# Local attention: scaling the queries on POOL with the keys, and a new order of copies and projections

## The reference, cut to what matters

```
h = shift_token(x)                       # half of the features from the token before
q, k, v = split(h @ wqkv)                # 8 heads of 64
q = l2norm(q) * qs;  k = l2norm(k) * ksc
q, k = rotary_xpos(q, k)                 # q*cos*scale + rotate_half(q)*sin*scale; k with 1/scale
...
sim = (8 * q) @ k.T                      # each window sees itself and the window before
attn = softmax(where(mask, -max, sim))
x = x + (attn @ v) @ wo
h = shift_token(x)
mu = h.mean(-1);  var = h.var(-1)        # for the feed-forward half that follows
```

## Time and profile before

| what | us |
|---|---|
| median of 3 runs | 1599.19 |
| profiled execution, its own time | 1601.15 |
| its span in the profile | 1599.4 |
| first local attention, start to the end of its last copy | 742.1 to 1084.1 |
| second local attention | 1163.6 to 1506.3 |
| PE busy / DVE busy / ACT busy / POOL busy, whole span | 1303.0 / 1178.1 / 1009.1 / 787.2 |

### The profile page before, as it was taken

One profiled execution on the slowest core, in us unless ns is written; L12 is line 12 of the kernel. 1 busy time (PEld: TensorE's weight loads), 2 busy tenths in 40 slices (PEclk: granted clock), 3 DMA queues, 4 the chain that ended last, 5 costly groups with the idle time before them and its releaser, 6 DMA issues. The chain is left out here.

```text
span 1599.4 us, 26941 instructions
## 1 busy us (share of the span) xinstructions
PE 1303.0 (81%) x9092; PEld 610.4 (38%) x9156; DVE 1178.1 (74%) x2033; ACT 1009.1 (63%) x2284; POOL 787.2 (49%) x957
## 2 busy tenths in 40 slices
PE   3489989989989785785799999877968999998596
PEld 1122222322222122453455555542325555555243
DVE  5778888888888663325788888858648888888493
ACT  3246766666666564233789998844248899888422
POOL 4566666767666201112767776710057677665000
PEclk9579999999999998887999999988979999999698
DMA  3523333333333201000111111101011111110001
GB/s 101 99 56 59 72 60 74 60 71 63 62 65 60 47 1 52 1 1 22 31 25 28 28 25 25 28 1 43 0 37 25 25 31 24 25 25 18 0 0 55
DMA packets 161404, 60.94 MB, mean 38 GB/s; under 512 B 139722, under 2 KB 153076, under 8 KB 161268
## 3 DMA queue, kind: packets, MB, share of 16 engines
q1 hardware_dynamic: 161268, 59.22, 17.6%
HBM read 8.73 MB, written 2.10 MB: 7 GB/s over the span
## 5 line engine op out<-in xcount | busy, mean ns | idle before, releaser
L639 DVE TENSOR_REDUCE row_max<-max_ps 128x2 f32<-128x1024 f32 x256 | 312.8, 1222 | 71.0 <-PE max_ps L451 69.6
L691 ACT ACTIVATE prob<-scores_ps 128x1024 f32<-128x1024 f32 x256 | 262.2, 1024 | 148.2 <-PE scores_ps L431 144.7
L1677 POOL TENSOR_TENSOR la_turned<-la_raw,lw_rot 128x1024 f32<-128x1024 f32 x64 | 150.7, 2354 | 287.0 <-ACT la_raw L1569 154.4
L1558 ACT ACTIVATE la_s<-la_s,la_bias,la_inv 128x128 f32<-128x128 f32 x512 | 223.0, 440 | 7.7 <-DVE la_bias L1471 7.4
L1314 PE MATMUL la_ring<-lw_wqkv,la_hT 128*128 128x512 f32 x384 | 203.9, 642 | 24.9 <-ACT la_hT L1553 13.4
L431 PE MATMUL scores_ps<-stack 128*128 128x512 f16 x512 | 155.8, 386 | 41.8 <-ACT prob L691 41.1
L1683 POOL TENSOR_TENSOR la_turned<-la_turned,la_swapped 128x1024 f32<-128x1024 f32 x64 | 150.5, 2352 | 5.0
L465 PE MATMUL heads_ps<-prob,v_pad 128*32 128x512 f32 x1024 | 137.4, 609 | 1.1 <-ACT prob L691 1.1
L451 PE MATMUL max_ps<-stack 24*128 24x512 f16 x512 | 102.5, 397 | 31.6 <-DVE row_max L639 19.2
L1446 DVE TENSOR_TENSOR la_swapped<-la_ring,lw_rot 128x256 f32<-128x256 f32 x256 | 91.9, 415 | 31.6 <-ACT la_raw L1569 20.5
L431 PEld LDWEIGHTS scores_ps<-stack 128*128 128x128 f16 x512 | 34.2, 97 | 208.7 <-ACT prob L691 161.7
(11 more groups left out here) (165 smaller groups left out, 2795.6 us busy)
## 6 DMA issues: line engine op xcount, KB each, us to landing
la_v_back<-la_v_own SPq DMA_DIRECT2D x112, 128.0 KB, 2.3
X<-in_x SPq DMA_DIRECT2D x8, 256.0 KB, 5.2
stack<-stack_tok SPq DMA_TRANSPOSE x128, 3.2
out<-X SPq DMA_DIRECT2D x8, 256.0 KB, 2.4
lw_wqkv<-in_wqkv SPq DMA_DIRECT2D x2, 768.0 KB, 4.7
stack<-shift_row SPq DMA_DIRECT2D x64, 2.0 KB
lw_rot<-in_rot SPq DMA_DIRECT2D x2, 512.0 KB, 6.4
lw_w<-in_fw SPq DMA_DIRECT2D x2, 341.0 KB
```

The costliest lines, as they stand in the source:

```text
L639: nc.vector.tensor_reduce(row_max[:, grp % 2, w // 2, :, w % 2], max_ps[:], AX.X, ALU.max).then_inc(max_made, 1)
L691: nc.scalar.activation(prob[:, c % 4, 2 * pr:2 * pr + 2, :], scores_ps[:], ACT.Exp, scale=1.0 / LOGIT_SCALE).then_inc(exp_made, 1)
L1558: ins = nc.scalar.activation(s_ps[:, place(h), :], s_ps[:, place(h), :], ACT.Exp, bias=bias[:, T % 2, h:h + 1], scale=inv[:, T % 4, h:h + ...
L1677: nc.gpsimd.tensor_tensor(spun, raw[:, T % 2].rearrange("p s (h f) -> p s h f", f=LD), rot[:, T % TPB, :, 0, :].unsqueeze(2).to_broadcast( ...
```

## The change

1/|q| is now multiplied into q on POOL, in one multiplication with the keys (`scale_turned`, 128x1024). So the exponentials take only a bias column, the maximum is itself that bias, and `maxima` has one instruction. Copies out of PSUM are shared out differently: `take_kT` and `take_out` go from DVE to ACT, `take_low` and `take_qT` from ACT to DVE (both halves of probT are now DVE's), `shift` from ACT to POOL. K is projected and rotated before Q. The order in every engine's slot is new; POOL polishes and scales tile N before it spins tile T. The subtraction of the mean, the squares of C and the copy of the variance come one slot later, and there is one slot more. TURN_Q now waits for `scaled` where it waited for `added_rot`.

The core of the diff:

```diff
-        T_LAST = NT + 7
+        T_LAST = NT + 8
-        PROJ_Q, PROJ_K, TURN_Q, PROJ_V, TURN_K = range(5)
+        PROJ_K, PROJ_Q, TURN_Q, PROJ_V, TURN_K = range(5)
...
             def transpose(T, use):
-                if use == TURN_Q:
-                    pe.wait_ge(added_rot, T + 1)
-                else:
-                    pe.wait_ge(scaled, T + 1)
+                pe.wait_ge(scaled, T + 1)
...
             def slot(n):                                   # PE
                 T, R, U, O = (tile_or_none(n - x) for x in (0, 2, 3, 4))
+                if O is not None:
+                    prob_turn(O, 0)
+                    prob_turn(O, 1)
+                if T is not None:
+                    project(T, PROJ_K)
+                if U is not None:
+                    scores(U)
                 if T is not None:
                     project(T, PROJ_Q)
-                    project(T, PROJ_K)
-                if O is not None:
-                    prob_turn(O, 0)
-                if U is not None:
-                    scores(U)
-                if R is not None:
-                    transpose(R, TURN_Q)
-                if O is not None:
-                    prob_turn(O, 1)
-                if T is not None:
-                    project(T, PROJ_V)
-                if R is not None:
-                    transpose(R, TURN_K)
                 b = ended(n - 7)
...
                 if O is not None:
                     weigh(O, 0)
+                if R is not None:
+                    transpose(R, TURN_Q)
+                if T is not None:
+                    project(T, PROJ_V)
+                if R is not None:
+                    transpose(R, TURN_K)
+                if O is not None:
                     weigh(O, 1)
...
             def maxima(T):
                 dve.wait_ge(s_filled, T + 1)
+                if T - 1 > 0:
+                    dve.wait_ge(exp_made, T - 1)
                 nc.vector.tensor_reduce(neg_max[:, T % 2], s_ps[:], AX.X, ALU.max, negate=True
                                         ).then_inc(max_made, 1)
-                dve.wait_ge(max_made, T + 1)
-                dve.wait_ge(inv_made, T + 1)
-                if T - 1 > 0:
-                    dve.wait_ge(exp_made, T - 1)
-                nc.vector.tensor_tensor(bias[:, T % 2].rearrange("p (c e) -> p c e", e=2),
-                                        neg_max[:, T % 2].rearrange("p (e c) -> p c e", e=2),
-                                        inv[:, T % 4, 0:LH].rearrange("p (c e) -> p c e", e=2),
-                                        ALU.mult).then_inc(bias_made, 1)
...
             def exps(T, e):
                 for h in range(e, LH, 2):
                     ins = nc.scalar.activation(s_ps[:, place(h), :], s_ps[:, place(h), :], ACT.Exp,
-                                               bias=bias[:, T % 2, h:h + 1], scale=inv[:, T % 4, h:h + 1],
+                                               bias=neg_max[:, T % 2, place(h):place(h) + 1],
                                                accum_out=sums[:, T % 2, place(h):place(h) + 1])
...
-            def scale_keys(T):
+            def scale_turned(T):
                 pool.wait_ge(added_rot, T + 1)
                 pool.wait_ge(inv_made, T + 1)
-                heads = turned[:, T % 2, 1].rearrange("p (h f) -> p h f", f=LD)
+                heads = turned[:, T % 2].rearrange("p s (h f) -> p (s h) f", f=LD)
                 nc.gpsimd.tensor_tensor(heads, heads,
-                                        inv[:, T % 4, LH:2 * LH].unsqueeze(2).to_broadcast([P, LH, LD]),
+                                        inv[:, T % 4].unsqueeze(2).to_broadcast([P, 2 * LH, LD]),
                                         ALU.mult).then_inc(scaled, 1)

+            def shift(b):
+                pool.wait_ge(x_added, b + 1)
+                pool.wait_ge(scaled, min((b + 1) * TPB + 4, NT))
+                if b > 0:
+                    pool.wait_ge(c_made, b)
+                x = batch_at(XT, b)
+                nc.gpsimd.tensor_copy(shifted[0:64, :], x[0:64, :]).then_inc(sh_made, 1)
+                pool.wait_ge(sh_made, 2 * b + 1)
+                nc.gpsimd.tensor_copy(shifted[64:P, 1:S], x[64:P, 0:S - 1]).then_inc(sh_made, 1)
+                pool.wait_ge(sh_made, 2 * (b + 1))
...
             def slot(n):                                   # POOL
                 T, N = tile_or_none(n), tile_or_none(n - 1)
+                if N is not None:
+                    polish(N)
+                    scale_turned(N)
+                if ended(n - 5) is not None:
+                    shift(ended(n - 5))
                 if T is not None:
                     spin(T)
-                if N is not None:
-                    polish(N)
-                    scale_keys(N)
```

More of the change, by code:

```diff
@@ L1438, in rotate @@
                 r = ring_index(T, use)
[L1439 removed]
+                dve.wait_ge(raw_made, 2 * T + 2 - side)
                 if T > 0:
@@ L1485, in share, with take_probT, take_qT @@
                                         ALU.mult).then_inc(shared, 1)
-            def take_high(T):
-                dve.wait_ge(pT_filled, 2 * T + 2)
+            def take_probT(T, half):
+                dve.wait_ge(pT_filled, 2 * T + half + 1)
                 if T > 0:
                     dve.wait_ge(o_filled, 2 * T)
[L1491 to L1508, removed]
+                heads = slice(4 * half, 4 * half + 4)
+                nc.vector.tensor_copy(probT[:, heads], pT_ps[:, heads]).then_inc((pT_low, pT_high)[half], 1)
+            def take_qT(T):
+                r = ring_index(T, TURN_Q)
+                dve.wait_ge(ring_filled, ring_count(T, TURN_Q))
+                if T - 1 > 0:
+                    dve.wait_ge(s_filled, T - 1)
+                nc.vector.tensor_copy(qT[:, T % 2].rearrange("p c q -> p (c q)"), ring_ps[:, r % 2, :]
+                                      ).then_inc(qT_made, 1)
             def slot(n):
-                T, N, R, U, O, out = (tile_or_none(n - x) for x in (0, 1, 2, 3, 4, 5))
+                T, N, R, U, O = (tile_or_none(n - x) for x in (0, 1, 2, 3, 4))
                 if O is not None:
@@ L1514, in slot @@
                     share(O, 1)
[L1515 to L1525, removed]
-                if N is not None:
-                    norms(N)
-                b = ended(n - 6)
+                b = ended(n - 7)
                 if b is not None:
@@ L1533, in slot @@
                                             ALU.subtract).then_inc(c_made, 1)
+                if O is not None:
+                    take_probT(O, 0)
+                    take_probT(O, 1)
+                if N is not None:
+                    norms(N)
+                if U is not None:
+                    maxima(U)
+                if T is not None:
+                    rotate(T, 1)
+                    rotate(T, 0)
                 b = ended(n - 5)
@@ L1538, in slot @@
                     nc.vector.tensor_tensor(x, m_ps[:], x, ALU.add).then_inc(x_added, 1)
+                if R is not None:
+                    take_qT(R)
             run(dve, slot)
@@ L1624, in slot @@
                     nc.scalar.activation(squares[:], raw[:, N % 2], ACT.Square).then_inc(sq_made, 1)
-                if O is not None:
-                    take_low(O)
-                if R is not None:
-                    take_qT(R)
                 if n % TPB == 1 and n + 3 < NT:
@@ L1631, in slot @@
                 if T is not None:
-                    take_values(T)
-                if U is not None:
-                    act.wait_ge(bias_made, U + 1)
-                    exps(U, 0).then_inc(exp_half, 1)
-                    exps(U, 1).then_inc(exp_made, 1)
-                b = ended(n - 6)
+                    take_raw(T, 1)
+                b = ended(n - 7)
                 if b is not None:
@@ L1644, in slot @@
                     inverse_norms(N)
-                b = ended(n - 5)
-                if b is not None:
-                    shift(b)
-                b = ended(n - 7)
+                b = ended(n - 8)
                 if b is not None:
@@ L1651, in slot @@
                     nc.scalar.activation(batch_at(VAR, b), m_ps[:], ACT.Copy).then_inc(var_made, 1)
+                if T is not None:
+                    take_raw(T, 0)
+                if U is not None:
+                    act.wait_ge(max_made, U + 1)
+                    exps(U, 0).then_inc(exp_half, 1)
+                    exps(U, 1).then_inc(exp_made, 1)
+                if T is not None:
+                    take_values(T)
+                if R is not None:
+                    take_kT(R)
+                if O is not None:
+                    take_out(O)
             run(act, slot)
```

46 lines of the change are left out of this document (18 added, 28 removed).

## The result

The changed kernel took 1612.37 us (median of 7 runs, 1605.08 to 1613.70); the kernel before took 1600.25 us (median of 7, 1598.80 to 1604.78). The ratio is 1.0063, 95% interval 1.0044 to 1.0082: slower. The forecast was 1577, faster, with a range of 1560 to 1610.

What follows compares the result with a forecast made beforehand. No engine saturated: a loop of waits through V's copy and the exponentials, 8.75 us a plain slot, bound it. Savings -1.2-2.3-5.5-0.25-1.3-0.7 = -11.25 us a layer, -22.5 for both, gave 1577 us, range 1560 to 1610.

Steps and rivals of the forecast that it cites:

- The new loop: Walk through local attention's slot in the new order: exponentials 8.42 us apart in a plain slot, where they were 8.75.
- norms at 5.35, 1.82 long: DVE's norms start 5.35 us after the exponentials and take 1.82, so maxima start at 7.17.
- 8.63, 8.80 and 8.42: Intervals between exponentials in us: after the slot with C, with the VAR copy, and plain.
- POOL becomes the bound: Rival: a POOL scale above 2.35 us makes POOL's round pass 8.42; about 1607 us, slower; chance 0.08.
- The column: Dropping the scale column from ACT's exponentials saves 0.09 us each, 0.72 for the eight of a tile.
- The column is free: Rival: exponentials stay 0.435 us apart without the scale column, the loop is 9.14; 1610 us, slower; chance 0.12.
- The loop through scores, 7.98: Loop from exponentials through share, probability transpose, K, scores and maxima to exponentials: 7.98 us, under the 8.42.
- 0.36 until PE's first scores matmul: In the kernel before, the step of its 8.75 us loop from DVE's multiply to PE's scores: 0.36 us.
- PE order. No instruction comes or goes: Part of the change on PE: the order alone changes, no instruction is added or removed.
- 10.57 forecast: Interval between exponentials after the output projection, whose eight matmuls stand after Q on PE: 10.57 us.
- The ends: Outside the middle batches, a layer: first exponentials -1.2 us, first five intervals -2.3, last piece -0.25, -1.3 and -0.7.
- the norms loop of the forecast: Plain slot: ACT's copies and squares, then DVE's norms and maxima, set the exponentials 8.42 us apart.

Runs made afterwards that it cites:

- a_noclip: Changed kernel without DVE's clip (maximum of the norms' sums of squares with 1e-24), its factor -0.5 made elsewhere; 1575.12 us, ratio 0.9838 to the kernel before.
- a_turn3: Changed kernel, clip kept, with three buffers of `turned` instead of two, so POOL's spin waits for an older transpose of k; 1583.75 us, ratio 0.9886.
- a_split4: Changed kernel, clip kept, with POOL's add of spin in four instructions of 128x256 instead of one of 128x1024; 1580.53 us, ratio 0.9863.
- a_noclip_col: a_noclip with a scale column of ones put back into the exponentials; 1614.69 us, ratio 1.0078 to the kernel before.
- a_col: Changed kernel, clip kept, with a scale column of ones put back into the exponentials; 1627.12 us, ratio 1.0168 to the kernel before.
- a_noclip_pe: a_noclip with PE reordered: K and Q projected together first, then both probability transposes, scores, both halves of weigh; 1623.96 us, ratio 1.0138 to the kernel before.

## Why the prediction was wrong, by its own steps

- **The step that failed** is in "The new loop": "norms at 5.35, 1.82 long (915.93 to 917.75)". 1.25 of it is the reduction, which stayed at 1.21 us; 0.57 was taken for the clip's own length. It was what POOL's product had left to run. In the new order the clip meets POOL's add, and from reduction to maxima it is 2.28 (877.85 to 880.13). I priced a wait as work, and moved it along with its instruction. Of the 2.18 us by which a batch (38.60) is above its forecast (36.42), 2.01 go with the clip (36.59 in a_noclip). Reading DVE's timeline against POOL's would have shown it: in the slot of the earlier trace rows, in the line left out there, the clip ran from 917.18 for 0.65, to 917.83, and POOL's product ended at 915.44+2.36 = 917.80; `bias` on 8 elements, with two SBUF operands too, took 0.17 at 914.32, when POOL was idle. The clip of that slot, from DVE's timeline of the kernel before:

```profile
917.18 0.65 DVE L1459 SCALAR_TENSOR_TENSOR la_sumsq<-la_sumsq,la_minus_half 128x16 f32<-128x16 f32 x1
```

- **What stood in its place** is a loop that the prediction hadn't drawn: spin, clip, maxima, rotations, q's transpose, V, k's transpose, spin: 9.07 in each of the three slots for which 8.63, 8.80 and 8.42 were forecast. a_turn3 cuts its last edge, a_split4 shortens its first, a_noclip takes out the link; each gives 29 to 37 us.
- **The rival "POOL becomes the bound"** named the engine and put 1607, but for a scale above 2.35. The scale is 1.90, the lower bound taken as forecast and not the 2.35 that the price of an element spoke for, and POOL still has 1.1 us of waits in a plain slot. It was right about the place and wrong about the mechanism.
- **The column**: 0.09 each, as forecast (0.342 between starts for 0.435). "The column is free" fell. a_noclip_col shows it at full price where the exponentials bind, a_col at a third of it where they don't.
- **The loop through scores, 7.98**, left out raw Q: from scores to exponentials it is 3.00, not 2.73. It also left out a matmul: scores begin with two matmuls of the band mask, and in the trace of the kernel before the first of them has no record (x1 at 920.30). So the 1.41 starts some 0.2 late, and "0.36 until PE's first scores matmul" is that much too long. Before the change the two errors cancel; behind K, with no wait to hide it, it is 1.08 from K to the recorded one in a_noclip for 0.91 forecast. The changed kernel's trace has both, 0.86 behind K:

```profile
877.55 0.59 PE L1331 MATMUL la_s<-lw_band,lw_identb 128*128 128x512 bf16 x2
```

Measured without the clip: 8.45. So the second loop was nearer than I said, by chance at the height of the first.
- **"PE order. No instruction comes or goes"** was costed at nothing. PE's busy time rose by 2.3 us a batch in the traces; 0.9 of that is the band matmul without a record (0.31 from the recorded one to the products before, 0.53 after, four times a batch), so some 1.5 are left. In V's place the next matmul begins 0.96 after it for 0.86, the halves of weigh take 0.62 each for 1.08 together. In the slot of the output projection this is the bound, PE without a gap: 11.1 without the clip for 10.57 forecast. What each switch of kind costs was not measured by itself, and that switches are the cause is not shown: a_noclip_pe, with K and Q together and weigh in one piece, is still busy 35.8.
- **The ends.** Outside the five middle batches the forecast took 5.75 us off each layer. Measured it is 1.9 more in layer 1 and 2.2 less in layer 2: the first five intervals took 45.8 and 46.3 for 42.1, and the first exponentials came 1.2 later and 1.6 earlier than before, counted from the layer's start, for 1.2 earlier.
- With the clip out, a batch is 36.6 for 36.42, and the kernel takes 1575 for 1577. That is near, but partly luck: the loop that gives 8.45 there is the one through scores and raw Q, not the norms loop of the forecast, which without the clip's 0.57 would have been shorter.

## What to carry to other kernels

A length in a profile can be a wait. Where an instruction is long for its elements, or has two lengths, look for rows of another engine that end with it, before moving it. Tiny DVE operations of the tied kinds (below) stand badly on a critical path beside long POOL instructions: fold them into the neighbours, or cut the POOL instruction they meet into shorter ones. When an order is turned round, list the loops again with every in-order predecessor (raw Q before the exponentials), not only the data they need.

## What the runs showed of the hardware

- The clip, with two SBUF operands or as an fp32 tensor_scalar with one, ends 0.02 to 0.05 us after the POOL instruction that ran when it came: 16 elements took 0.17 alone and up to 2.16 beside POOL in the changed kernel. The reduction of 1024 elements from SBUF (1.21), the reciprocal of 4 elements from SBUF (0.17) and the operations with an operand in PSUM (0.69) ran beside the same POOL instructions at their usual length. POOL's lengths didn't change.
- POOL's multiply with a broadcast column takes 1.04 for 512 elements and 1.90 for 1024, below the 2.35 of a product or sum of two full operands.
- The same matmuls show 36.6 us of PE busy time a batch for 34.3 in the other order; some 0.9 of it is the unrecorded band matmul, so the real growth is about 1.5 us, 4%. Why the order costs this is open.
